# The inverse roots of the token normalisations: a power on GpSimd and one Newton round on VectorE, in place of a bit trick and three rounds

## What is computed

```python
t = _to_tokens(x)
t = t + _L1_attn_ref(_ln_t(t), L1_attn_w_qkv, L1_attn_w_out, L1_attn_b_out)
t = t + _L1_ffn_ref(_ln_t(t), L1_ffn_gate_w, L1_ffn_gate_b, L1_ffn_w1, L1_ffn_b1, L1_ffn_w2, L1_ffn_b2)
def _ln_t(v, eps=1e-05):
    m = jnp.mean(v, axis=-1, keepdims=True)
    s = jnp.var(v, axis=-1, keepdims=True)
    return (v - m) / jnp.sqrt(s + eps)
```

## Time and profile before

| | before |
|---|---|
| median of 3 runs | 729.14 us (729.09 to 731.33) |
| profiled execution | 731.6 us, span 729.9 us |
| TensorE busy | 608.2 us, 83% of the span |
| VectorE busy | 465.5 us, 64% |
| ScalarE busy | 318.1 us, 44% |
| GpSimd busy | 213.2 us, 29% |
| mean granted clock of TensorE | 0.929 of full speed |

### The profile page before, as it was taken

How to read it: one execution, slowest core, us unless ns; L and a number is a source line. 1 busy time by engine, 2 the same in 40 slices (tenths; PEclk the granted TensorE clock), 3 DMA queues, 4 the chain that set the end, 5 groups by cost and what they waited for, 6 DMA issues and landing times.

```text
span 729.9 us, 14331 instructions
## 1 busy us (share of the span) xinstructions
PE 608.2 (83%) x3834; PEld 535.4 (73%) x3835; DVE 465.5 (64%) x1556; ACT 318.1 (44%) x626; POOL 213.2 (29%) x193
## 2 busy tenths in 40 slices
PE   6652589989888985148999999999999999999982
PEld 3541477767777974037998898899899899899872
DVE  1788699898989885614565564564565555555650
ACT  1645577867676642013333343333334333333330
POOL 5230121212746666711122122122221221221221
PEclk9887699999999996559999999999999999999995
DMA  9380887868786972411255372744626528322211
GB/s 280 127 329 16 314 305 274 315 238 306 272 314 217 356 297 80 134 53 32 45 153 189 55 284 44 245 97 105 231 44 165 181 37 280 65 38 45 31 15 14
DMA packets 50487, 120.82 MB, mean 166 GB/s; under 512 B 7564, under 2 KB 39184, under 8 KB 44304
## 3 DMA queue, kind: packets, MB, share of 16 engines
q1 hardware_dynamic: 30128, 98.07, 37.2%
q0 software_dynamic: 11136, 14.00, 11.5%
q10 hardware_dynamic: 9184, 8.28, 4.2%
HBM read 68.22 MB, written 52.11 MB: 165 GB/s over the span
## 4 chain that ended last, share of the span: by engine, by line
PE 58%; DVE 23%; issue 7%; ACT 5%; POOL 2%; DVEq 1%; DMA 1%; ACTq 0%; SPq 0%; POOLq 0%
PE ps L843 42%; PE ps L870 6%; DVE wset L1114 4%; DVE stt L1023 2%; POOL rows_by_expert L440 2%; PE ps L674 2%; PE ps L836 2%; PE ps L741 2%; PE ps L730 1%; DVE img L1108 1%; ACT xh L540 1%; DVE tc L1014 1%; PE ps L778 1%; ACT img L534 1%; DVE bst L993 1%
## 5 line engine op out<-in xcount | busy, mean ns | idle before, releaser
L462 POOL DMA_INDIRECT out<-ys,xr x56 | 86.7, 1548 | 318.8 <-DVE ys L1393 248.0
L843 PE MATMUL ps<-wset,hTh 128*128 x896 | 163.6, 283 | 7.1 <-DVE hTl L1361 7.0
L843 PEld LDWEIGHTS ps<-wset,hTh 128*128 128x128 f32 x896 | 141.8, 190 | 15.0 <-issue 11.0
L843 PE MATMUL ps<-wset,xrTh 128*128 x448 | 147.5, 411 | 0.0
L635 ACT ACTIVATE hb<-hb 128x512 f32<-128x512 f32 x112 | 70.5, 632 | 140.6 <-DVE hb L1382 140.6
L843 PE MATMUL ps<-wset,hTl 128*128 x448 | 126.4, 282 | 0.0
L641 ACT CAST hTh<-ps 128x512 fp32r<-128x512 f32 x112 | 60.1, 589 | 102.0 <-PE ps L870 101.6
L1388 DVE TENSOR_TENSOR yb<-ps,bset 128x256 f32<-128x256 f32 x56 | 23.8, 425 | 124.2 <-PE ps L843 124.2
L843 PEld LDWEIGHTS ps<-wset,xrTh 128*128 128x128 f32 x448 | 81.2, 191 | 15.6
L843 PE MATMUL ps<-wset,xrTl 128*128 x224 | 89.5, 400 | 0.0
L1382 DVE TENSOR_TENSOR hb<-ps,bset 128x512 f32<-128x512 f32 x112 | 76.0, 685 | 17.2 <-PE ps L843 17.2
(11 more groups left out here) (181 smaller groups left out, 943.9 us busy)
## 6 DMA issues: line engine op xcount, KB each, us to landing
split_weights<-wset SPq DMA_DIRECT2D x16, 2048.0 KB, 7.4
wset<-split_weights SPq DMA_DIRECT2D x32, 1024.0 KB, 7.2
wset<-in_ew SPq DMA_DIRECT2D x16, 1024.0 KB, 10.2
xr<-rows_by_expert ACTq DMA_DIRECT2D x56, 132.5 KB, 2.1
bset<-in_eb SPq DMA_DIRECT2D x8, 640.0 KB, 8.9
img<-in_x SPq DMA_DIRECT2D x8, 392.0 KB, 6.4
out<-img SPq DMA_DIRECT2D x16, 196.0 KB
rows_by_expert<-rows,slot POOLq DMA_INDIRECT x64, 3.4
```

The costliest lines, as they stand in the source:

```text
L462: pool.indirect_dma_start(out, bass.IndirectOffsetOnAxis(xr[:, r % XR, C + E:ROW].bitcast(U32), 0), ys[:, r % YS, :], None, compute_op=ALU ...
L843: last = pe.matmul(dst, rows_k[:, k * 128:(k + 1) * 128], wset[:, bass.ds(column(k) + rest, width)], start=(k == 0 and n == 0), stop=(k == ...
```

## The change

GpSimd gets a step of its own in each slot with a normalisation: the power of minus one half of variance plus epsilon, by an elementwise instruction with a constant tile of -0.5. VectorE keeps eps, skips two turns of its generator, waits for the power, and does one Newton round and the shift. The seed, the guess and two rounds are gone: 5 instructions on VectorE in place of 13. In GpSimd's slot the power comes first, and the four scatters are parted: two behind norm_bias and two behind soft_q, where all four were behind soft_q.

```diff
     "ctx": {"vec": ["ctx0", "ctx1"], "act": ["proj"], "pe": ["ctx", "proj"]},
     "out": {"vec": ["add"], "pe": ["out"]},
     "norm2": {"vec": ["stat0", "stat1", "agg0", "agg1"], "act": ["norm0", "norm1", "xT"], "pe": ["xT", "logits"]},
-    "root": {"vec": ["eps", "seed", "guess"] + [f"newton{k}{m}" for k in range(3) for m in range(3)] + ["shift"]},
+    "root": {"vec": ["eps", "square", "slope", "root", "shift"], "pool": ["power"]},
     "route": {"vec": ["bias", "max", "sub", "sum", "rec", "prob", "top0", "top1", "top2", "top3",
                       "at0", "at1", "at2", "at3", "den", "atf", "denr", "one1", "one2", "both", "run0", "comb",
                       "run1", "scale", "run2", "run3", "pos", "pos1", "pos2", "slot1", "slot2", "slots"],
@@ -115,6 +115,7 @@
...
         iotf = sb("iotf", [128, 64])
         expert_id = sb("expert_id", [HALF, 4, E])
         expert_row = sb("expert_row", [HALF, 4, E])
+        power = sb("power", [HALF, 2, 2])
         tokid_i = sb("tokid_i", [HALF, TILES], I32)
         xT = sb("xT", [128, 2, 2, HW])
         stt = sb("stt", [HALF, 2, 2, 2, 6])
@@ -372,6 +373,7 @@
                 built(pool.memset(t[:, :], v))
             built(pool.memset(run[:, :, :, :], 0.0))
             built(pool.memset(lt[:, :, :], 1.0))
+            built(pool.memset(power[:, :, :], -0.5))
             built(pool.iota(tokid_i[:, :], pattern=[[HALF, TILES]], base=0, channel_multiplier=1))
             built(pool.iota(iot, pattern=[[1, 64]], base=0, channel_multiplier=0))
             built(pool.affine_select(out=ident[:, :], in_=ident[:, :], compare_op=ALU.not_equal, fill=1.0,
@@ -424,31 +426,42 @@
                                    qr[:, p, 2, :].unsqueeze(2).to_broadcast([HALF, 2 * HEADS, DH]),
                                    ALU.mult).then_inc(S["soft"]["pool"], 1)
 
-            def send_rows(g, j):
+            def first_roots(n):
+
+                W, q = slice(0 if n - LAG["norm"] < B else 1, 2 if n >= LAG["norm2"] else 1), n % 2
+                wait_for(pool, "root", "vec", "eps", n - 1)
+                pool.tensor_tensor(sm[:, q, 1, W, :], sm[:, q, 0, W, :], power[:, W, :],
+                                   ALU.pow).then_inc(S["root"]["pool"], 1)
+
+            def send_rows(g, j, h):
 
                 at = 2 * g % RING + j
-                if j == 0:
+                if j == 0 and h == 0:
                     wait_for(pool, "route", "vec", "scale", g)
                     wait_for(pool, "norm2", "act", "norm1", 2 * g + 1)
                     pool.tensor_copy(rows[:, at:at + 2, :, C + E:ROW].bitcast(I32).rearrange("p i j r -> p (i j r)"),
                                      tokid_i[:, 4 * g:4 * g + 4]).then_inc(s_tok, 1)
                     pool.wait_ge(s_tok, g + 1)
                     wait_for(pool, "route", "vec", "slots", g)
-                for h in range(2):
-                    for k in range(2):
-                        t = 2 * j + h
-                        pool.indirect_dma_start(norm_rows, bass.IndirectOffsetOnAxis(slot[:, g % 2, k, t:t + 1], 0),
-                                                rows[:, at, h, :], None).then_inc(s_rows[g % (RING // 2)], 16)
+                for k in range(2):
+                    t = 2 * j + h
+                    pool.indirect_dma_start(norm_rows, bass.IndirectOffsetOnAxis(slot[:, g % 2, k, t:t + 1], 0),
+                                            rows[:, at, h, :], None).then_inc(s_rows[g % (RING // 2)], 16)
 
             pool.wait_ge(s_wa, 9 * 16)
             for n in range(SLOTS_A):
+                if LAG["norm"] <= n < B + LAG["norm2"]:
+                    first_roots(n)
                 if 0 <= n - LAG["norm"] < B:
                     norm_bias(n - LAG["norm"])
+                if n >= ROUTE_LAG + 2:
+                    send_rows((n - ROUTE_LAG - 2) // 2, n % 2, 0)
                 if 0 <= n - LAG["soft"] < B:
                     soft_q(n - LAG["soft"])
                 if n >= ROUTE_LAG + 2:
-                    send_rows((n - ROUTE_LAG - 2) // 2, n % 2)
-            send_rows(B // 2 - 1, 1)
+                    send_rows((n - ROUTE_LAG - 2) // 2, n % 2, 1)
+            for h in range(2):
+                send_rows(B // 2 - 1, 1, h)
 
 
             pool.wait_ge(s_res, 16 * B)
@@ -1042,21 +1055,16 @@
                     wait_for(dve, "norm2", "act", "norm1", n - 2 - LAG["norm2"])
                 root(V.tensor_scalar(v, mv[:, W, q, :, 1], LN_EPS, None, ALU.add))
                 yield
+                yield
+                yield
+                wait_for(dve, "root", "pool", "power", n - 1)
+                root(V.tensor_tensor(t, y, y, ALU.mult))
+                yield
                 dve.wait_ge(S["root"]["vec"], r[0])
-                root(V.tensor_scalar(y.bitcast(I32), v.bitcast(I32), 1, -1, ALU.logical_shift_right, ALU.bitwise_xor))
+                root(V.scalar_tensor_tensor(out=t, in0=t, scalar=-0.5, in1=v, op0=ALU.mult, op1=ALU.mult))
                 yield
                 dve.wait_ge(S["root"]["vec"], r[0])
-                root(V.tensor_scalar(y.bitcast(I32), y.bitcast(I32), MAGIC, None, ALU.add))
-                for _ in range(3):
-                    yield
-                    dve.wait_ge(S["root"]["vec"], r[0])
-                    root(V.tensor_tensor(t, y, y, ALU.mult))
-                    yield
-                    dve.wait_ge(S["root"]["vec"], r[0])
-                    root(V.scalar_tensor_tensor(out=t, in0=t, scalar=-0.5, in1=v, op0=ALU.mult, op1=ALU.mult))
-                    yield
-                    dve.wait_ge(S["root"]["vec"], r[0])
-                    root(V.scalar_tensor_tensor(out=y, in0=t, scalar=1.5, in1=y, op0=ALU.add, op1=ALU.mult))
+                root(V.scalar_tensor_tensor(out=y, in0=t, scalar=1.5, in1=y, op0=ALU.add, op1=ALU.mult))
                 yield
                 dve.wait_ge(S["root"]["vec"], r[0])
                 root(V.scalar_tensor_tensor(out=m, in0=mv[:, W, q, :, 0], scalar=-1.0, in1=y,
@@ -1438,7 +1446,7 @@
             vec_slot(SLOTS + 1, 1)
 
 
-NCONST = 25
+NCONST = 26
 WPARTS = 4
 LOAD_E = 16 * (WPARTS + 1)
 NCW = 6
```

More of the change, by code:

```diff
@@ L1044, in inverse_roots @@
                 yield
-                dve.wait_ge(S["root"]["vec"], r[0])
-                root(V.tensor_scalar(y.bitcast(I32), v.bitcast(I32), 1, -1, ALU.logical_shift_right, ALU.bitwise_xor))
+                yield
+                yield
+                wait_for(dve, "root", "pool", "power", n - 1)
+                root(V.tensor_tensor(t, y, y, ALU.mult))
                 yield
                 dve.wait_ge(S["root"]["vec"], r[0])
-                root(V.tensor_scalar(y.bitcast(I32), y.bitcast(I32), MAGIC, None, ALU.add))
-                for _ in range(3):
-                    yield
-                    dve.wait_ge(S["root"]["vec"], r[0])
-                    root(V.tensor_tensor(t, y, y, ALU.mult))
-                    yield
-                    dve.wait_ge(S["root"]["vec"], r[0])
-                    root(V.scalar_tensor_tensor(out=t, in0=t, scalar=-0.5, in1=v, op0=ALU.mult, op1=ALU.mult))
-                    yield
-                    dve.wait_ge(S["root"]["vec"], r[0])
-                    root(V.scalar_tensor_tensor(out=y, in0=t, scalar=1.5, in1=y, op0=ALU.add, op1=ALU.mult))
+                root(V.scalar_tensor_tensor(out=t, in0=t, scalar=-0.5, in1=v, op0=ALU.mult, op1=ALU.mult))
+                yield
+                dve.wait_ge(S["root"]["vec"], r[0])
+                root(V.scalar_tensor_tensor(out=y, in0=t, scalar=1.5, in1=y, op0=ALU.add, op1=ALU.mult))
                 yield
```

## The result

| | before | changed |
|---|---|---|
| median | 730.24 us (729.09 to 731.64, 4 runs) | 738.95 us (737.42 to 740.37, 4 runs) |
| ratio to before | | 1.0118, 95% interval 1.0101 to 1.0136 |
| profiled execution, span | 731.6, 729.9 us | 738.05, 736.3 us |
| GpSimd busy | 213.2 us | 227.9 us |

The forecast was 732.4 against a median of 729.14, so +3.25; the medians moved by +8.7, the profiled executions by +6.45 (the one of before lies 1.4 above its median). The side is right and the range holds the time, but the size is half or less.

A forecast was written before the change was run, and what follows sets the result against it. VectorE and ScalarE in turn bound the attention stage, then GpSimd's queue from slot 11; -1.15 us plus powers of 3.0 and 1.4 gave +3.25, so 732.4 from a median of 729.14, range 726 to 740.5.

The forecast's parts named there:

- What bounds the kernel; slots 1 to 9: Attention stage: VectorE and ScalarE wait on each other; the earlier shift gains 10.2 us, so slot 10 starts at 155.6.
- The power's price: Duration of GpSimd's power: 0.5 us for 98x4, 0.35 for 98x2, between bounds 0.19 and 1.27; ten powers add 4.4.
- The pause: GpSimd's 5.3 us before its first scatter in slot 10, hidden before, now delays slot 11's power.
- rival B: The pause of 5.3 us before the first scatter does not fall on the ring: -2.05 us, 727.1; chance 0.2.
- rival C: The power's first use, in slot 1, pays a pause like the first scatter's: 2.7 us more, 735.1; chance 0.1.
- Rival D: The power is evaluated row by row, some microseconds each; at 2 us each the time is 753; chance 0.07.
- The ring: From slot 10, each power waits behind GpSimd's bias, scatters and q, which wait for the last power: 12.7 us plus power.
- T(11): Moment when VectorE has slot 11's power, forecast at 177.25 us plus one power's duration; other slots' numbers are read likewise.
- The pause is elsewhere: Sign of a wrong forecast: GpSimd's pause of 5.3 us does not stand before slot 10's first scatter.
- the stage ends 10 us or more earlier: Sign of a wrong forecast: GpSimd reaches the power before VectorE asks, so the attention stage ends that much earlier.
- VectorE's waits from slot 11 on: Sign for the forecast: VectorE waits for GpSimd's power, about 6 us in slot 11 and least before odd slots.

The follow-up runs named there:

- Power twice: Changed kernel with each power issued twice on GpSimd, the first time into a spare tile; first chip, 749.53 us, ratio 1.0276.
- the multiply: Changed kernel with a multiplication by 0.5 in place of the power, everything else the same; first chip, 729.78 us, ratio 0.9995.
- before's order: Kernel before with a slot's four scatters issued in the next slot ahead of the bias, which leaves GpSimd's order unchanged; second chip, 739.99 us, ratio 1.0009.
- early-power pair: Changed kernel with the power only in slots 1 to 9: scatters parted (first chip, 728.86 us) or all behind q (second chip, 730.24 us).
- early power, parted: Changed kernel with the power on GpSimd in slots 1 to 9 only, VectorE's three rounds from slot 10, scatters parted; first chip, 728.86 us, ratio 0.9992.

## Why the prediction was right in kind and short in size

**What bounds the kernel; slots 1 to 9.** Right. Slot 10 started at 154.04 where 155.6 was forecast: 11.8 us gained, not 10.2. The single slots were less exact: slot 6 gained 2.2 (2.0), slots 7 and 8 1.1 and 0.9 (1.6 each), slot 9 2.5 (2.05), and slots 2 and 4, given 0 and 0.1, gained 1.05 and 1.65. TensorE's turn closes them, as said.

**The power's price**: the first failed term. "Between ends so far apart I take the geometric middle, 0.5, and for two columns 0.35." It is 1.04 and 0.74; six and four of them make 9.2 us instead of 4.4. The true value lay inside the bounds (0.19 to 1.27), close to the upper one. Power twice (+10.6 us for 8.8 of powers) and the multiply (−9.2 for 7.1) show that it passes to the end in full or more. The estimate by the Trainium skill (GPSIMD Engine Reference, section 3), 0.3, is contradicted by the 1.04 of a power; for the multiply, 0.21 us, it is not far.

**The pause**: the second failed step. "Now slot 11's power is behind it." It would have been, but the pause was gone: from the copy's start to the first scatter's it took 0.53 us instead of the 5.3 worked out. That was rival B's premise, and B's conclusion (faster) fell to the price. Slot 1 gained 1.25 us of the 1.3 forecast and its power took 0.78 us, so rival C (a first-use pause of the power) is out; the 6 us that the Trainium skill, GPSIMD Engine Reference, section 2.1, gives for a first call show at no power here. Rival D, a power of 2 us or more, is out at 1.04.

**The ring.** Right in kind: power, then ScalarE's normalisation (5.6 us as forecast: 172.61 to 178.20), bias, two scatters, q, two scatters, power, without a gap. Two pieces were taken too short: bias to first scatter takes 1.49 us, not 1.24, and that scatter 1.33, not 1.27. With the measured powers put into the prediction's chain:

| start of | by the prediction, powers as measured | measured | difference |
|---|---|---|---|
| T(11) | 178.3 | 172.6 | −5.7 (early gain −1.6, pause −4.8, rest +0.7) |
| T(16) | 247.5 | 243.4 | −4.1 |
| T(17) | 259.7 | 256.0 | −3.7 |
| T(18) | 268.5 | 266.2 | −2.3 |
| T(19) | 280.0 | 278.2 | −1.8 |
| pair 7's scatters | 303.73 + 8.05 = 311.8 | 310.4 | −1.4 |

So the sum reads: −1.15 forecast apart from powers, +9.2 for the powers, −1.6 for an early gain of 11.8 instead of 10.2, −4.8 for the absent pause, and +5.0 for a ring and late slots that were each a little longer than worked out. That is +6.65 against a stage end moved by 6.64 and a span by 6.4. The forecast's +3.25 held four errors, of +4.8, −1.6, −4.8 and +5.0, and that the time still fell into the range is in part luck, since they nearly cancel in pairs. With the price, the early gain and the pause as measured, and the ring as the prediction worked it out, the sum would be +1.65, no change clear of noise; it is the longer ring that makes the loss clear.

**VectorE against GpSimd.** This is not in the prediction at all: with more work on GpSimd and q moved, some of VectorE's smallest instructions stall. In the changed kernel six of them take 0.8 to 1.6 us from slot 10 on, each ending with a GpSimd instruction. In slot 12 the negative (L1080) takes 1.61 us and ends with q; how much of it hides in the wait for the power was not worked out.

```profile
181.49 1.61 DVE L1080 TENSOR_SCALAR kx<-kx 128x2 f32<-128x2 f32 x1
```

**The signs of a wrong forecast.** "The pause is elsewhere" came true; "the stage ends 10 us or more earlier" did not. Of the signs for it, VectorE's waits from slot 11 on and the shortest ones in odd slots are there, but slot 11's is 1.5 us, not 6, and the steps are 14.0 and 14.4 us, not 12.7 to 13.5.

**What stays open.** It stays open why nine instructions more on GpSimd remove the pause: shown is only that the power is not needed for it. It is open, too, why the kernel before takes 9 us longer on the second chip, and the changed one 2.6 less, so that the change's sign turns. In the trace of before's order there, the slots up to 16 start within 2 us of the first chip's; then VectorE's and ScalarE's timelines show idle times that the first chip's do not have:

```profile
267.51 0.59 ACT L579 COPY ekt<-ps 98x512 f32<-98x512 f32 x1 [2.60 <-remote]
...
273.43 0.69 DVE L1109 TENSOR_TENSOR img<-ps,img 98x512 f32<-98x512 f32 x1 [1.33 <-issue]
...
282.23 0.17 DVE L1044 TENSOR_SCALAR sm<-mv 98x2 f32<-98x2 f32 x1 [1.18 <-DVE mv L1028]
```

Neither question was taken further. The early-power pair (parted and together) did not run on one chip either: its 6.5 us are read from slots up to 16, where the chips agree within 2.3 us, and the two stood within 0.2 us at slot 10.

## What to carry to other kernels

An operation moved to an engine that is idle on average costs what stands ahead of it in that engine's order: here the same power cost +9 us behind four scatters (against a multiply in its place), and with the power ahead of them the kernel was 15.5 us faster than before. When an unknown price is multiplied by ten on a closed ring, measure it by itself first, or let its upper bound set the forecast. Before explaining a difference of 1%, run both versions on one chip; a comparison over two chips gave here a cause with the wrong sign.

## What the runs showed of the hardware

- GpSimd's elementwise power takes 1.04 us for 98x4 and 0.74 for 98x2 (changed kernel), a multiply of either size 0.21, a copy of 98x4 0.19. Two powers of 98x2 that ran beside VectorE's split of 128x2048 took 2.6 us (power twice, slots 1 and 2).
- A VectorE instruction of 0.17 us on 128x2 numbers took up to 1.73 us (early power, parted) where a GpSimd elementwise instruction ran beside it, and ended within 0.05 us of that one's end.
- The issue of a scatter, 0.96 us, took 2.96 where VectorE's split of 128x2048 ran beside it (kernel before, at 222.68). In all fourteen traces the sixteen scatters that began during a split took 2.1 to 3.0 us, and no other took over 1.5. In the changed kernel none began during one.
- GpSimd's pause before the first scatter, 5.1 to 6.2 us in four traces, was absent in every kernel with nine or more GpSimd instructions added ahead of it, powers or multiplies.
- The kernel before took 729.7 us on one chip and 739.1 on another; the changed kernel took 739.0 and 736.3.
